# Four-layer graph network on one core: in the expansion stage GpSimd makes the normalised copies of odd groups, and ScalarE and VectorE share the copies of z

## The reference

```python
h = jnp.maximum(_layernorm(x, axis=-1), 0.0)
x = x + _L1_gnn_ref(h, adj, L1_gnn_W1, ...)
# in it:
A_hat = A_norm * dinv[:, None] * dinv[None, :]
agg = jnp.einsum('nm,bmd->bnd', A_hat, features)
x = agg.reshape(-1, d)
h = jax.nn.relu(_batchnorm(x @ W1.T + b1, g1, be1))   # 128 -> 256 features
out = h @ W2.T + b2
out = _batchnorm(out, g2, be2)
```

## Time and profile before

| | us |
|---|---|
| median of 3 runs | 1357.95 |
| lowest, highest | 1357.65, 1361.84 |
| the profiled execution | 1358.01 |
| its span, first to last instruction | 1356.3 |
| the expansion stage in it, from GpSimd's last scale (667.4) to VectorE's last statistics | about 59 |

### The profile page before, as it was taken

One profiled execution on the slowest core, in us unless ns is written; L12 is line 12 of the kernel. 1 busy time (PEld: TensorE's weight loads), 2 busy tenths in 40 slices (PEclk: granted clock), 3 DMA queues, 4 the chain that ended last, 5 costly groups with the idle time before them and its releaser, 6 DMA issues.

```text
span 1356.3 us, 21468 instructions
## 1 busy us (share of the span) xinstructions
PE 1009.0 (74%) x5490; PEld 632.3 (47%) x5490; DVE 983.1 (72%) x3979; ACT 714.8 (53%) x2021; POOL 380.3 (28%) x1171
## 2 busy tenths in 40 slices
PE   3666666666644234049989789999999999699997
PEld 1444444445532113027554478444566444366665
DVE  7777788888887998986787865444455555677776
ACT  2333344444424243716466676775666554477774
POOL 4035555566634756200100033101023310100000
PEclk9999999999999999579999799999999999899999
DMA  5000000000010000000000000000000000000101
GB/s 159 1 0 1 1 1 1 1 1 1 1 41 17 1 1 1 1 0 1 1 0 0 0 1 1 0 0 0 0 0 0 1 0 0 1 17 23 31 23 32
DMA packets 16667, 12.47 MB, mean 9 GB/s; under 512 B 665, under 2 KB 14530, under 8 KB 16578
## 3 DMA queue, kind: packets, MB, share of 16 engines
q1 hardware_dynamic: 16578, 11.49, 3.1%
HBM read 7.23 MB, written 4.19 MB: 8 GB/s over the span
## 4 chain that ended last, share of the span: by engine, by line
PE 58%; DVE 26%; issue 7%; ACT 4%; POOL 2%; DMA 1%; DVEq 1%; ACTq 0%; POOLq 0%
PE P L1483 33%; PE P L715 14%; DVE arena L370 2%; DVE arena L490 2%; PE P L1643 2%; DVE arena L495 1%; DVE arena L488 1%; DVE bcol L389 1%; PE P L1636 1%; PE P L1649 1%; PE P L1614 1%; DVE scal L358 1%; DVE bst_all L951 1%; PE P L1632 1%; PE P L1653 1%
## 5 line engine op out<-in xcount | busy, mean ns | idle before, releaser
L1483 PE MATMUL P<-arena,WT 128*128 128x336 f32 (+2 forms) x792 | 300.5, 539 | 3.6 <-POOL arena L928 2.3
L1483 PEld LDWEIGHTS P<-arena,WT 128*128 128x128 f32 x792 | 149.1, 190 | 148.9 <-issue 117.2
L715 PE MATMUL P<-arena 1*128 1x127 f32 (+62 forms) x504 | 150.6, 428 | 89.2 <-DVE arena L370 87.0
L1378 ACT ACTIVATE arena<-P,bl 128x512 f32<-128x512 f32 (+1 forms) x252 | 152.5, 635 | 65.5 <-PE P L1483 59.5
L715 PEld LDWEIGHTS P<-arena 1*128 1x128 f32 x504 | 122.1, 308 | 131.0 <-DVE arena L367 120.5
L654 ACT ACTIVATE arena<-arena 1x127 f32<-1x127 f32 (+62 forms) x126 | 32.2, 256 | 165.4 <-DVE arena L381 155.1
L940 POOL COPY arena<-arena 128x336 f32<-128x336 f32 (+1 forms) x40 | 43.4, 1098 | 211.1 <-PE P L1483 146.7
L201 POOL TENSOR_SCALAR lf<-lf 1x1 f32<-1x1 f32 x210 | 87.7, 418 | 21.9
L715 PE MATMUL P<-arena,Ib 128*128 128x46 bf16 (+1 forms) x318 | 35.5, 273 | 63.8 <-ACT arena L684 63.1
L715 PE MATMUL P<-I,bcol 128*1 128x128 f32 (+62 forms) x252 | 47.7, 286 | 35.5 <-DVE bcol L389 35.4
L1382 ACT ACTIVATE arena<-arena 128x512 f32<-128x512 f32 (+1 forms) x72 | 40.8, 578 | 55.8 <-DVE arena L1152 48.3
(11 more groups left out here) (529 smaller groups left out, 2592.2 us busy)
## 6 DMA issues: line engine op xcount, KB each, us to landing
out_dram<-xN SPq DMA_DIRECT2D x16, 256.0 KB, 2.3
Wn<-in_L_gnn_Wih_dram SPq DMA_DIRECT2D x4, 256.0 KB, 2.8
Wn<-in_L_gnn_Whh_dram SPq DMA_DIRECT2D x4, 256.0 KB, 2.8
Wqkv<-in_L_gnn_W_dram SPq DMA_DIRECT2D x1, 192.0 KB
W1n<-in_L_gnn_W_dram SPq DMA_DIRECT2D x1, 128.0 KB
W2n<-in_L_gnn_W_dram SPq DMA_DIRECT2D x1, 128.0 KB
Wg<-in_L_gnn_Wg_dram SPq DMA_DIRECT2D x2, 64.0 KB
adj<-in_adj_dram SPq DMA_DIRECT2D x1, 64.0 KB, 1.8
```

The costliest lines, as they stand in the source:

```text
L715: def mm(o,l,r,start=True,stop=True): return t.matmul(o,lhsT=l,rhs=r,start=start,stop=stop)
L1378: act(s.gt[u][gate][:,0:cols],P[4*u+gate][:,0:cols],f,bias=s.bl[:,4*(p-1)+gate:4*(p-1)+gate+1]).then_inc(ev('lstm_gates'),1)
L1483: def mm(o,l,r,start=True,stop=True,**k): return t.matmul(o,lhsT=l,rhs=r,start=start,stop=stop,**k)
```

## The change

- The normalised copies of odd groups (`hb[1]`) move from ScalarE to GpSimd: new function `gpsimd_h`, four `tensor_scalar` of 128x128 (multiply and add with a scale and an offset per node) and one `tensor_scalar` of 128x512 (maximum with 0, in place). It is called for groups 1 and 3 after the first portion of scales, and for groups 5 to 15 after the second portion.
- The copy of z of odd groups (`P[1]` to `zb[1]`) moves from VectorE to ScalarE (`odd_copy`). VectorE keeps the even one (`expand_copy`).
- The semaphores are split: `expand_h` and `expand_mixed` now count even groups alone, `expand_h_odd` and `expand_mixed_odd` odd ones. TensorE waits for each in the order that it had.

```diff
--- before.py
+++ after.py
@@ -285,7 +285,10 @@
         e(ts(near[:,:],far[:,:],-1.0,1.0,ALU.mult,ALU.add))
         tt(gap[:,:],gap[:,:],near[:,:],ALU.add).then_inc(ev('eigen_from_gpsimd'),1)
         net.gpsimd_chain=e
-        for first,last in ((0,FIRST_GROUPS),(FIRST_GROUPS,NG)): net.gpsimd_scales(eng,2,first,last)
+        net.gpsimd_scales(eng,2,0,FIRST_GROUPS)
+        for g in (1,3): net.gpsimd_h(eng,g)
+        net.gpsimd_scales(eng,2,FIRST_GROUPS,NG)
+        for g in range(5,NG,2): net.gpsimd_h(eng,g)
         for first,last in ((0,FIRST_GROUPS),(FIRST_GROUPS,NG)): net.gpsimd_scales(eng,3,first,last)
         net.gpsimd_gcn(eng)
         net.gpsimd_windows(eng)
@@ -951,6 +954,18 @@
         v.bn_stats(s.bst_all[:,bass.ds(g*GB*6+b*6,6)], x[:,bass.ds(g*C+b*N,N)]).then_inc(s.ev('layer_stats'),1)
   def rsqrt(s,v,c,var,tmp,out,k):
     pass
+  def gpsimd_h(s,eng,g):
+
+    e=s.gpsimd_chain
+    if g<4: eng.wait_ge(s.ev('layer_scale'),2)
+    else: eng.wait_ge(s.ev('layer_scale'),3)
+    if g>1: eng.wait_ge(s.ev('expand_product1'),g-1)
+    else: eng.wait_ge(s.ev('spectral_product1'),NG)
+    for b in range(GB):
+        q=g*GB+b
+        step=e.mark(eng.tensor_scalar(s.hb[1][:,b*N:(b+1)*N],s.xN[:,q*N:(q+1)*N],s.rsd[:,q:q+1],s.nmr[:,q:q+1],ALU.mult,ALU.add))
+    e.wait(step)
+    eng.tensor_scalar(s.hb[1][:,:],s.hb[1][:,:],0.0,None,ALU.max).then_inc(s.ev('expand_h_odd'),1)
   def gpsimd_scales(s,eng,k,first,last):
 
     ev=s.ev
@@ -1048,10 +1063,9 @@
     g4=lambda t: t.rearrange("p (b d) -> p b d",d=N)
 
     v.sem_inc(ev('spectral_x'),2)
-    def copy_z(stage,it):
-        for u in range(2):
-            v.wait_ge(ev(stage+'product1'),2*it+u+1)
-            v.tensor_copy(s.zb[u][:,:],P[u][:,:]).then_inc(ev(stage+'mixed'),1)
+    def expand_copy(it):
+        v.wait_ge(ev('expand_product1'),2*it+1)
+        v.tensor_copy(s.zb[0][:,:],P[0][:,:]).then_inc(ev('expand_mixed'),1)
     def spectral_copy(g):
         v.wait_ge(ev('spectral_product1'),g+1)
         v.tensor_copy(s.spectral_zb[g%4][:,:],P[g%4][:,:]).then_inc(ev('spectral_mixed'),1)
@@ -1068,7 +1082,7 @@
         for g in quad:
             v.wait_ge(ev('spectral_product4'),g+1)
             tt(X(g),X(g),P[4+g%4][:,:],ALU.add).then_inc(ev('spectral_x'),1)
-        if it==NQ-1: copy_z('expand_',0)
+        if it==NQ-1: expand_copy(0)
         for g in quad:
             if it<NQ-1: spectral_copy(g+4)
             spectral_stats(g)
@@ -1082,7 +1096,7 @@
             ts(Hb,P[4+u][:,:],s.bcol('L1_gnn_b1',2)[:,1:2],None,ALU.add).then_inc(ev('expand_hidden'),1)
             v.wait_ge(ev('expand_hidden'),2*it+u+3)
             v.bn_stats(s.bst2[:,bass.ds(6*NG+g*6,6)],Hb).then_inc(ev('batch_stats'),1)
-            if more and u==1: copy_z('expand_',it+1)
+            if more and u==1: expand_copy(it+1)
             v.wait_ge(ev('expand_hidden_first'),2*it+u+3)
             v.bn_stats(s.bst2[:,bass.ds(g*6,6)],R1[:,bass.ds(g*C,C)]).then_inc(ev('batch_stats'),1)
     with v.Fori(0,2) as it: hidden_b(it,True)
@@ -1316,13 +1330,18 @@
     s.layer_roots(a,2,0)
     s.first_scales(a,2)
     a.wait_ge(ev('spectral_product1'),NG)
+    def odd_copy(it):
+        a.wait_ge(ev('expand_product1'),2*it+2)
+        act(s.zb[1][:,:],P[1][:,:],ACT.Copy).then_inc(ev('expand_mixed_odd'),1)
     def hidden_b(it,more):
         for u in range(2):
             g=2*it+u
-            ahead(it,u,'expand_',more)
+            if u==0: ahead(it,u,'expand_',more)
             a.wait_ge(ev('expand_product2'),2*it+u+1)
             act(R1[:,bass.ds(g*C,C)],P[2+u][:,:],ACT.Identity,bias=s.bcol('L1_gnn_b1',2)[:,0:1]).then_inc(ev('expand_hidden_first'),1)
-    s.act_ln(a,0,'expand_')
+        if more: odd_copy(it+1)
+    s.act_ln(a,0,'expand_',(0,))
+    odd_copy(0)
     hidden_b(0,True)
     s.layer_roots(a,2,1)
     with a.Fori(1,5) as it: hidden_b(it,True)
@@ -1504,10 +1523,10 @@
     t.wait_ge(ev('spectral_x'),NG)
     with t.Fori(0,NP) as it:
         for u in range(2):
-            t.wait_ge(ev('expand_h'),2*it+u+1)
+            t.wait_ge(ev('expand_h_odd' if u else 'expand_h'),it+1)
             mix(P[u],s.hb[u],s.AhT[:,:]).then_inc(ev('expand_product1'),1)
         for u in range(2):
-            t.wait_ge(ev('expand_mixed'),2*it+u+1)
+            t.wait_ge(ev('expand_mixed_odd' if u else 'expand_mixed'),it+1)
             t.wait_ge(ev('expand_hidden'),2*it+u+1)
             t.wait_ge(ev('expand_hidden_first'),2*it+u+1)
             mm(P[2+u][:,:],s.W1T[:,0,:],s.zb[u][:,:])
```

## The result

The changed kernel took 1365.92 us (median of 6 runs, 1364.38 to 1366.97) against 1359.37 (6 runs, 1357.65 to 1361.84): a ratio of 1.0049, 95% interval 1.0036 to 1.0062. It is slower by 6.6 us where 7.1 were forecast, at 1365.9 where 1365.1 was; the median of the kernel before is 1.4 us higher here than in the three runs that the forecast started from. The profiled execution has a span of 1364.3 us, 8.0 more than before.

The account below looks back on a forecast made before the run. No engine was full; a loop of waits between VectorE and TensorE set 6.48 us a pair. From 1358.0, less 1.4 (earlier first product2), plus 6.8 (stall at pair 2) and 1.7 (clock): 1365.1 us, range 1361.5 to 1370.

Follow-up runs that it names:

- e3: Kernel before, with ScalarE making the odd copy of z and TensorE's wait for the copy put last of three; ratio 0.9987 to the kernel before.
- e6: Changed kernel with TensorE's loop over the pairs written out, so all its waits have constants; pairs of 6.48 us, ratio 1.0043 to the kernel before.
- e9: Changed kernel with VectorE making both copies of z and GpSimd copying group 5 ahead of the scales that wait for the reciprocal; ratio 1.0011 to the kernel before.

## What to carry to other kernels

When no engine is full, find the loop of waits, write down what stands in each engine's list between its two ends, and ask of an edit only whether it takes something from there: a copy taken from outside the loop became 0.6 us of idle (e3: 1.60 ahead of the even L1081, 1.00 before), while one copy moved by one place won 0.8 us a pair. Before work goes to an idle in-order engine, look at what that engine waits for between its old instructions, because its waits now hold up whoever needs the new work: here one wait of 11.8 us that had cost nothing became the whole loss. And when waits stand together in a loop, ahead of the work that is the critical one, it is worth trying one count for all of them: a second count ahead of it cost 0.16 us a pair here.

## What the runs showed of the hardware

- GpSimd's `tensor_scalar` has very different prices. Multiply-and-add over 128 columns with two per-partition operands took 0.454 us; a single maximum over 512 columns 1.486 (2.9 ns a column); maximum and add over 512 columns 1.919 (3.7 ns a column). The Trainium skill (GPSIMD Engine Reference, section 4.1, Engine selection) calls one-input work roughly line rate. For the maximum the rows disagree, by the 1.486 us; for multiply-and-add with constants, at 0.86 ns for each further column (0.205 us for 16, 0.301 for 128), they come nearer.
- The Trainium skill (SBUF — State Buffer, its notes on the shared port pair) has GpSimd blocked only by VectorE operations in a two-port mode or with two inputs in on-chip memory. The trace of the changed kernel agrees as far as it goes: beside statistics with one input and moves from PSUM, GpSimd's eight maxima lie within 1485 to 1491 ns.
- A semaphore that VectorE's sequencer raises behind 16 queued statistics (3.18 us of work) reached TensorE 1.06 us after the first had started (e3): the sequencer runs ahead of the engine. Whether its own pace or a bound on its lead sets the 1.06 isn't shown.
- A wait of one register count, followed by two of another, cost TensorE 0.16 us a pass ahead of the critical matmul, of 6.48 (the changed kernel); written out with constants it cost nothing (e6). Two counts elsewhere in the loop body cost nothing either (e3, e9).
- The granted clock isn't settled by one pause. In the head it fell to 0.50 in the trace of before and stayed at 1.00 in e9, both with TensorE idle for 1.68 us ahead of the first product2.
